# Weight-value products over two slots; the f gate straight from PSUM, with the low half of h made by a scan

## What is computed

```
x = x + _L0_cond_ref(x, cond, ...)      # attention, projection, feed-forward
x = x + _L1_cond_ref(x, cond, ...)      # LSTM over the 512 rows

    scores = jnp.einsum('bhqd,bhkd->bhqk', qt, kt) / math.sqrt(HD)
    attn = jax.nn.softmax(scores, axis=-1)
    out_h = expmap0(jnp.einsum('bhqk,bhkd->bhqd', attn, vt))
    ...
    def step(carry, xw_t):
        prev_h, prev_c = carry
        a = xw_t + prev_h @ Wh
        i = sigmoid(a[:, 0:H]);     f = sigmoid(a[:, H:2*H])
        o = sigmoid(a[:, 2*H:3*H]); g = tanh(a[:, 3*H:4*H])
        next_c = f * prev_c + i * g
        next_h = o * tanh(next_c)
        return (next_h, next_c), next_h
```

## Time and profile before

| | |
|---|---|
| median of 3 runs | 1871.57 us (1865.92 to 1875.25) |
| profiled execution | 1874.7 us |
| its span, first to last instruction | 1872.9 us |
| block 0, attention part | 244 to 333 us |
| blocks 1 to 3 with LSTM steps | 470 to 1562 us |
| tail, 128 steps alone | 1562 to 1865 us |
| PE, DVE, ACT busy | 65%, 64%, 51% of the span |

### The profile page before, as it was taken

How to read it: one execution, slowest core, us unless ns; L and a number is a source line. 1 busy time by engine, 2 the same in 40 slices (tenths; PEclk the granted TensorE clock), 3 DMA queues, 4 the chain that set the end, 5 groups by cost and what they waited for, 6 DMA issues and landing times.

```text
span 1872.9 us, 60357 instructions
## 1 busy us (share of the span) xinstructions
PE 1217.5 (65%) x21103; PEld 985.0 (53%) x21103; DVE 1190.8 (64%) x6785; ACT 948.8 (51%) x3287; POOL 254.4 (14%) x674
## 2 busy tenths in 40 slices
PE   4666677276777557867776498677754975444444
PEld 4544455145666445656665366566653664444443
DVE  6465555311788765648887666588875755666665
ACT  0333378434677644547775455577753543333332
POOL 4222200332000032210000413000013220000000
PEclk9666655588555557965555588655555986555555
DMA  8000000000000000000000000000000000000000
GB/s 261 0 0 0 0 1 0 1 0 1 3 0 0 2 2 2 2 26 3 0 1 2 2 2 2 26 2 0 1 2 2 3 2 13 0 0 0 0 0 13
DMA packets 14556, 17.86 MB, mean 10 GB/s; under 512 B 3348, under 2 KB 13208, under 8 KB 14360
## 3 DMA queue, kind: packets, MB, share of 16 engines
q1 hardware_dynamic: 10248, 10.50, 1.8%
q10 hardware_dynamic: 4112, 4.86, 0.9%
HBM read 13.25 MB, written 2.10 MB: 8 GB/s over the span
## 4 chain that ended last, share of the span: by engine, by line
PE 41%; DVE 24%; ACT 13%; issue 12%; POOL 6%; DMA 1%; POOLq 1%; ACTq 1%; DVEq 1%; SPq 0%
PE psum L721 20%; DVE cnew L1269 4%; ACT tC L967 4%; DVE h L1277 3%; PE psum L695 3%; DVE h L1280 3%; PE psum L704 3%; DVE gO L1263 3%; POOL sc L226 3%; PE psum L663 3%; PE psum L553 3%; PE psum L673 2%; DVE cadd L1266 2%; PE psum L605 2%; PE psum L590 2%
## 5 line engine op out<-in xcount | busy, mean ns | idle before, releaser
L721 PE MATMUL psum<-h,wh 128*128 128x8 f16 x16384 | 514.9, 168 | 405.3 <-DVE h L1280 387.3
L721 PEld LDWEIGHTS psum<-h,wh 128*128 128x128 f16 x16384 | 480.6, 103 | 522.4 <-DVE h L1280 489.9
L961 ACT ACTIVATE tA<-gA 128x16 f32<-128x16 f32 x512 | 110.8, 216 | 482.9 <-DVE gA L1259 482.1
L1259 DVE TENSOR_REDUCE gA<-psum 128x16 f32<-128x32 f32 x512 | 97.3, 190 | 177.5 <-PE psum L721 176.8
L590 PE MATMUL psum<-qbd,kT 128*128 128x256 f16 x512 | 151.7, 401 | 24.3 <-ACT weights L847 21.7
L967 ACT ACTIVATE tC<-cnew 128x8 f32<-128x8 f32 x512 | 108.9, 213 | 90.6 <-DVE cnew L1269 40.6
L847 ACT ACTIVATE weights<-psum 128x512 f16<-128x512 f32 x256 | 152.2, 594 | 0.0
L1277 DVE TENSOR_TENSOR h<-oU,tC 128x8 f16<-128x8 f32 x512 | 89.1, 174 | 95.8 <-ACT tC L967 94.8
L605 PEld LDWEIGHTS psum<-vs,weights 128*128 128x128 f16 x2048 | 112.8, 111 | 29.5 <-issue 14.4
L1269 DVE TENSOR_TENSOR_SCAN cnew<-cmul,cadd 128x24 f32<-128x24 f32 x512 | 107.8, 211 | 27.0
L605 PE MATMUL psum<-vs,weights 128*128 (+1 forms) x2048 | 118.3, 198 | 8.6 <-DVE weights L342 8.5
(11 more groups left out here) (223 smaller groups left out, 2175.6 us busy)
## 6 DMA issues: line engine op xcount, KB each, us to landing
arena<-in_x_dram SPq DMA_DIRECT2D x4, 512.0 KB, 9.9
wf<-in_L_cond_w_f_dram SPq DMA_DIRECT2D x2, 1024.0 KB, 19.7
xs<-in_x_dram SPq DMA_DIRECT2D x4, 512.0 KB, 5.4
out_dram<-place SPq DMA_DIRECT2D x16, 128.0 KB, 2.1
arena<-in_L_cond_w_ada_dram ACTq DMA_DIRECT2D x1, 1536.0 KB
weights<-in_L_cond_Wh_dram ACTq DMA_DIRECT2D x1, 1024.0 KB, 14.6
gates<-in_L_cond_b_ada_dram ACTq DMA_DIRECT2D x8, 128.0 KB, 15.2
wx<-in_L_cond_Wx_dram SPq DMA_DIRECT2D x1, 1024.0 KB, 21.5
```

The lines of the kernel that those rows point to most:

```text
L721: last = mm(cols, wh16[:, half, kc, (g0 + g) * P:(g0 + g + 1) * P], h16[:, kc, :, :], start=False, stop=g == n - 1 and kc == KD - 1 and ha ...
```

## The change

There are two edits. In attention, `weighted` takes one head at a time: the first head's 8 matmuls stand in slot 2 hp + 4, the second's in slot 2 hp + 5, and both now stand ahead of the scores of their slot. `t_AV` is raised behind the second.

In the LSTM step, h lies in a tensor `hl` whose two halves are apart, each number the last of three. DVE writes the high half, and one scan of 24 elements over (-1, 0, hi) and (0, oU, tC) gives oU*tC - hi in every third place, the low half. The f32 product is made again for `hs`, at the end. The f bank has one column for each number: PE adds the products of the high half there as soon as `l_hi` comes (8 matmuls of 4 columns), and those of the low half between gates A and O (8 more). ACT reads the f gate from PSUM; the reduce to `gF` is gone. The step's matmuls become 40, of which 32 stand behind the wait for the low half.

```
-            def weighted(k, b, hp):
+            def weighted(k, b, hp, e):
+                if e == 0:
                     for half in range(2):
                         pe.wait_ge(s[f"t_l{half}"], HP * k + hp + 3)
...
             def pe_attention(k, b, q):
                 hp = q // 2
+                if 2 <= hp < HP + 2:
+                    weighted(k, b, hp - 2, q % 2)
                 if hp < HP:
                     scores(k, b, hp, q % 2)
-                if q % 2 == 0 and hp >= 2:
-                    weighted(k, b, hp - 2)
...
             def put_round(m, first):
-                for (bk, g0, n, made), read in zip(GATE_BANKS, ("l_gA", "l_gF", "l_gO")):
+                for (bk, g0, n, e), read in zip(GATE_BANKS, ("l_gA", "l_tF", "l_gO")):
...
             def pe_step(m, r, more=True):
+                both = lambda kc: hl[:, :, kc, :, 2].rearrange("p e b -> p b e")
+                pe.wait_ge(s["l_hi"], m)
+                gate_products(1, r, lambda kc: hl[:, 0, kc, :, 2])
                 pe.wait_ge(s["l_lo"], m)
+                gate_products(0, r, both).then_inc(s["l_A"], 1)
+                gate_products(1, r, lambda kc: hl[:, 1, kc, :, 2]).then_inc(s["l_F"], 1)
+                gate_products(2, r, both).then_inc(s["l_O"], 1)
...
-                act.wait_ge(s["l_gF"], m)
-                A(cmul[:, :, 1], gF[:], ACT.Tanh, scale=down).then_inc(s["l_tF"], 1)
+                act.wait_ge(s["l_F"], m)
+                A(cmul[:, :, 1], gate_cols(pF, 2, 1, r)[:, :, 0], ACT.Tanh, scale=down).then_inc(s["l_tF"], 1)
...
-                v.wait_ge(s["l_F"], m)
-                d.tensor_reduce(gF[:], gate_cols(pF, 2, r), axis=AX.X, op=ALU.add).then_inc(s["l_gF"], 1)
...
-                d.tensor_tensor(hi, by_k(oU), by_k(tC), ALU.mult).then_inc(s["l_hi"], 1)
-                d.tensor_tensor(h32[:], oU[:], tC[:], ALU.mult).then_inc(s["l_h32"], 1)
-                v.wait_ge(s["l_h32"], m)
-                d.tensor_tensor(lo, by_k(h32), hi, ALU.subtract).then_inc(s["l_lo"], 1)
+                d.tensor_tensor(hcol, by_k(oU), by_k(tC), ALU.mult).then_inc(s["l_hi"], 1)
+                v.wait_ge(s["l_hi"], m + 1)
+                d.tensor_tensor_scan(lo3, ot3[:].rearrange("p c e -> p (c e)"), hi3, 0.0, ALU.mult, ALU.subtract).then_inc(s["l_lo"], 1)
                 d.tensor_copy(cadd[:, :, 0:2], cnew[:, :, 2:3].to_broadcast([P, KD * B, 2])).then_inc(s["l_cc"], 1)
-                d.tensor_copy(hs[...], h32[:]...)
+                d.tensor_tensor(hs[...], by_k(oU).unsqueeze(3), by_k(tC).unsqueeze(3), ALU.mult).then_inc(s["l_hs"], 1)
```

More of the change, by code:

```diff
@@ L170, in bass_hyperbolic_block_then_lstm @@
         cnew = sb("cnew", [P, 8, 3])
-        tC = sb("tC", [P, 8])
+        oU, tC = ot3[:, :, 1], ot3[:, :, 2]
+        hcol, hi3, lo3 = hl[:, 0, :, :, 2], hl[:, 0].rearrange("p k b e -> p (k b e)"), hl[:, 1].rearrange("p k b e -> p (k b e)")
         unit = sb("unit", [P, GC])
@@ L593, in scores @@
                 last.then_inc(s[f"t_S{half}"], 1)
-            def weighted(k, b, hp):
[L597 to L607, removed]
+            def weighted(k, b, hp, e):
+                if e == 0:
+                    for half in range(2):
+                        pe.wait_ge(s[f"t_l{half}"], HP * k + hp + 3)
+                    if hp % (HP // 2) == 0:
+                        pe.wait_ge(s["t_o"], 2 * k + 1 + hp // (HP // 2))
+                h = 2 * hp + e
+                for kc in range(NB):
+                    for wl in range(2):
+                        last = mm(sums(h), weights[:, hp % 2, wl, kc, e * P:(e + 1) * P], tile_of(vs, b)[:, kc, h, :],
+                                  start=kc == 0 and wl == 0, stop=kc == NB - 1 and wl == 1, skip_group_check=True)
+                if e == 1:
+                    last.then_inc(s["t_AV"], 1)
             def pe_attention(k, b, q):
                 hp = q // 2
+                if 2 <= hp < HP + 2:
+                    weighted(k, b, hp - 2, q % 2)
                 if hp < HP:
                     scores(k, b, hp, q % 2)
-                if q % 2 == 0 and hp >= 2:
-                    weighted(k, b, hp - 2)
                 if q == LEAD + 1:
@@ L705, in put_gates, with gate_products @@
                    start=True, stop=True, skip_group_check=True)
             def put_round(m, first):
-                for (bk, g0, n, made), read in zip(GATE_BANKS, ("l_gA", "l_gF", "l_gO")):
+                for (bk, g0, n, e), read in zip(GATE_BANKS, ("l_gA", "l_tF", "l_gO")):
                     pe.wait_ge(s[read], m)
-                    put_gates(bk, g0, n, first)
+                    put_gates(bk, g0, n, e, first)
+            def gate_products(which, r, h_of):
+                bk, g0, n, e = GATE_BANKS[which]
+                for g in range(n):
+                    cols = gate_cols(bk, n, e, r)[:, g * B:(g + 1) * B, :]
+                    for kc in range(KD):
+                        for half in range(2):
+                            last = mm(cols, wh16[:, half, kc, (g0 + g) * P:(g0 + g + 1) * P], h_of(kc),
+                                      start=False, stop=g == n - 1 and kc == KD - 1 and half == 1, skip_group_check=True)
+                return last
@@ L767, in _ @@
             pe.wait_ge(s["l_x0"], 1)
-            for bk, g0, n, made in GATE_BANKS:
-                put_gates(bk, g0, n, 0)
+            for bk, g0, n, e in GATE_BANKS:
+                put_gates(bk, g0, n, e, 0)
             with pe.Fori(1, NB) as j:
@@ L966, in act_step @@
                 act.wait_ge(s["l_c"], m)
-                A(tC[:], cnew[:, :, 2], ACT.Tanh, scale=0.5).then_inc(s["l_tC"], 1)
+                A(tC, cnew[:, :, 2], ACT.Tanh, scale=0.5).then_inc(s["l_tC"], 1)
             act.wait_ge(s["l_init"], 2)
```

47 lines of the change are left out of this document (20 added, 27 removed).

## The result

The changed kernel takes 1901.82 us (median of 4 runs, 1898.1 to 1905.33), against 1871.83 of the kernel before on the same chip. The ratio is 1.0163, with a 95% interval of 1.0144 to 1.0181: slower by 1.6%. I had said 1871 us with a range of 1856 to 1886, so the time is outside it, and on the side to which I gave 0.20. The profiled span is 1900.2 us, 27.3 more than before.

The account below looks back on a forecast made before the run. No engine alone was taken as the bound: a closed chain of waits sets plain steps, PE some others. Terms -3.3 + 0.9 + 9.0 - 6.5 = +0.1 us on the runs' median 1871.7 gave 1871 us, range 1856 to 1886.

Parts of the forecast that it names:

- the side to which I gave 0.20: Whole kernel: slower, by the early matmuls or a late product; chance 0.20.
- Attention of blocks 1 to 3: Attention slots with LSTM steps: small step savings against costlier put slots, +0.3 us a block, +0.9 for three.
- Behind attention: Steps behind attention, blocks 1 to 3: 20 PE-bound steps a block cost +4.0, others save; +3.0 us a block, +9.0 together.
- a rival on the clock: PE's granted clock rises to 1.0 in attention and tail: 1831 us, or about 1850 if in attention alone; chance 0.06.
- Block 0: Attention without steps: ACT waits less for weight-value products, -6.5 us, bounds 0 and 10.3.
- Tail: Last 127 steps: 120 save 0.04 us each, 7 behind a put cost 0.22 each; together -3.3 us.
- The early matmuls aren't hidden even in the plain step: Between high half and gate A on PE: every step loses, 1884 to 1891 us; shares 0.20 with a late product.
- The change does not do what it says: Attention with steps: odd-slot products come too late and ACT stalls, 1881 us; left within the slower case, 0.20.
- The steps that I credit: The 320 steps credited with saving 0.04 us each; losing that saving was a bound of +12.8 us.

Follow-up runs that it names:

- e5_scan_spread: The changed kernel with the f bank as before (paired, reduce to `gF`, 32 matmuls a step); scan, `hl` and spread products stay: 1859.75 us, ratio 0.9933.
- e4_after_unrolled: The changed kernel with PE's loop over tiles in blocks 1 to 3 written out, same instructions and order: 1882.38 us, ratio 1.0044 to the kernel before.
- e6_before_unrolled: The kernel before with PE's loop over tiles in blocks 1 to 3 written out, same instructions and order: 1870.6 us, ratio 0.9984.

## Why the prediction was wrong

**The step that failed: "Attention of blocks 1 to 3", +0.3 a block.** It measured +6.50, +6.09 and +6.11. I costed the eight matmuls as time on PE, and I had the jumps of its loop nowhere in the sum. Each costs some 3.3 us (+2.07 and +1.15 in slots 19 and 20), and the six together 20. Written out, the same stage is -1.1 to -1.2 a block, so the rest of the stage was even better than forecast: the put step behind slot 15 is 3.80, not 4.0 (3.38 before), and normal slots save 0.05, not 0.04. That the size of the saving nearly came out is in part luck. The scan gives only 0.02 of the 0.04 that I worked out for it, and the 0.03 from the early matmuls and the f gate I had put at nothing.

The price of such a jump was in the trace of before. No jump of its loop over tiles stalls, but PE's loop over blocks, whose body is far longer (128 steps of 64 instructions are 8192 alone), jumps back twice, and the branch takes 3.58 and 3.88 us. The third branch leaves the loop. The line of the branch, and the load behind its first jump:

```profile
L770 PEldq COMPARE_BRANCH  x3: 79/3584/3881, 829.4 to 1559.9; - x3
```

```profile
833.20 0.93 PEld L721 LDWEIGHTS psum<-h,wh 128*128 128x128 f16 x32 [4.87 <-issue]
```

All 13 profiled kernels have these two long branches, 3.44 to 4.44 us each. So the rival that was missing could have been priced: a larger body may stall at its six jumps, at 3.4 to 3.7 us each over the usual 0.2, some 20 to 22 us. What the trace of before could not show is that the limit lies above 1627 and at or below 1755 instructions.

**"Behind attention", +3.0 a block, measured +7.96, +3.74, +7.80.** The price of a PE-bound step was right, their number was not: slots 79, 92, 95, 97, 99, 103 and 115 of block 1 are longer by 0.21 to 0.25, against my 0.20. But of the 21 steps of that block before which PE was late, eight (73, 101, 109, 117, 119, 122, 123, 125) changed by less than 0.1. The +3.74 of block 2 is near my number by luck: slot 103 is 1.39 shorter there, at a granted 1.00 instead of 0.69. What I missed is that the granted clock rises later: some 1.1 us in slots 74 to 76 of every block, and 1.2 or so more in slot 124 of two blocks. I did have a rival on the clock, but only as a rise in attention and the tail. It went the other way, and in another stage.

**Block 0, -6.5: the size was right, the working only in part.** It is -5.95, and -6.33 with the spread alone. ACT's waits for products between 244 and 333 us:

```profile
ACT tmp L856 <- PE psum L604: 5.4, 10, 0.9
ACT fT L856 <- PE psum L604: 1.7, 5, 0.4
```

They are 7.1 us, not the 3 that I named: before they were 10.3. So the stage got nearly as much shorter as forecast, but ACT's waits for products fell by only 3.2. ACT's three waits for scores, 1.2 in all before, are gone as well. No experiment took apart where the other 1.6 us come from, and that the size came out is in part luck.

**Tail, -3.3: right in kind, -4.81.** With the scan alone the tail gives -1.9 (e5_scan_spread), so the early matmuls and the f gate from PSUM, which I had as a loss of 1.5 behind the puts and otherwise nothing, give 2.9 together. The step behind a put is 0.23 longer (forecast 0.22), as the row of the step behind the 6 matmuls of the put has it: PE is late there as in the earlier trace rows.

```profile
1741.70 0.17 DVE L1287 TENSOR_TENSOR hl<-ot 128x8 f16<-128x8 f32 x1 [0.15 <-ACT ot L976]
...
1742.74 1.25 PE L720 MATMUL psum<-hl,wh 128*128 128x4 f16 x40
...
1744.80 0.17 DVE L1287 TENSOR_TENSOR hl<-ot 128x8 f16<-128x8 f32 x1
```

**The rivals.** "The early matmuls aren't hidden even in the plain step" gave 1884 to 1891, near the time but by a mechanism that is not there: the plain step is shorter. "The change does not do what it says" fell as well: with the loop written out attention is faster. The right rival was missing.

**My count of steps.** The steps that I credit are 120 in each of the tail and attention and 96 behind attention, 336 and not 320; it changes a bound by 0.6 us.

**Account.** Of the 30 us lost, the jumps are 19.4 (after less e4_after_unrolled, both timed). In the profiles they are 20.0 of 27.3, and the other 7.4 are +19.5 behind attention, less 10.8 of block 0 and the tail and 1.3 that attention gains outside the jumps. Block 1 as an example, +7.96: slots 74, 76, 120 and 124 are +3.74 (in 74, 76 and 124 mostly the clock, and 0.8 of it the matmuls themselves), the seven PE-bound slots above +1.64, and slots 93, 105, 111 and 126 +2.42. Of these, 105 was granted 0.67 instead of 1.00 and 111 0.69 instead of 0.77; for 93 and 126 the cause stays open.

## What to carry over

When an edit adds instructions to a loop, count the body of the loop on that engine before and after, and look at the instruction queue's packets on the page: here 1627 instructions on PE cost nothing, and 1691 (in four jumps of six) and 1755 (in all) cost 2 to 3.7 us and 9 packets for each jump that stalled. Read the time of the branch itself. A longer loop elsewhere in the kernel may already show what a stalled jump costs: here it did. An edit of matmul counts in a stage with f32 work can also move the point where the granted clock rises, so compare the clock over the same slots, not only the busy time. And test the parts of a change one by one: two of the three edits here (scan and spread) are worth 0.7% by themselves, and the third one, with what it does to the jumps and the clock, loses 2.3%.

## What the runs showed of the hardware

- PE's jump back in a loop: the branch takes 0.21 to 0.25 us at 1499 and 1627 instructions. At 1691 it takes 4.6 to 5.1 in two of three blocks and 0.22 to 0.24 in the third, with the same code. At 1755 it takes 3.3 to 3.9 in all 18 (three kernels), and at over 8192 3.4 to 4.4 in all 26. Why 1691 waits longer than 1755 stays open, and so does the second gap (1.65 in the changed kernel) that only kernels with 40 matmuls a step had.
- Code that is fetched without a jump costs nothing that can be seen: 142 packets instead of 110 in e6_before_unrolled, and 1870.6 us.
- At a granted 0.50, the 8 additional 4-column matmuls cost 0.21 in a PE-bound step; 4 columns instead of 8 saved nothing (0.026 each, where 8 columns take 0.027).
- A tanh of 128x8 from PSUM took 0.16 us, from a copy made by DVE 0.21.
- A scan of 24 elements that writes f16 with a stride of three took 0.21, as the f32 one.
